# Two weighted-latent products of a latent-attention kernel formed together in every second step, both halves of the second feed-forward layer in one step

## The reference

```python
xn = layernorm(x)
# attention on xn; it normalises again, with scale and bias, to h
c_q, c_kv = h @ w_down_q.T, h @ w_down_kv.T              # 64 latents each
q, k, v = c_q @ w_up_q.T, c_kv @ w_up_k.T, c_kv @ w_up_v.T   # 16 heads of 64
q, k = rope(q), rope(k)
attn = softmax(q @ k.T / 8)                              # 256 x 256 per head
a = (attn @ v) @ w_out.T + xn
# feed-forward with a spiking neuron
y = square(relu(xn @ W_fc.T)) @ W_proj.T
spikes = number of spikes in 5 steps of mem = 0.9*mem + y - reset
out = x + a + spikes / 5
```

## Time and profile before

| | |
|---|---|
| median of 3 executions | 1122.33 us (1120.78 to 1128.31) |
| profiled execution | 1125.72 us, its span 1123.8 us |
| TensorE clock granted, mean of the span | 0.987 of full speed |
| steps | 256, and 12 before the first; 8 a batch |

### The profile page before, as it was taken

How to read it: one execution, slowest core, us unless ns; L and a number is a source line. 1 busy time by engine, 2 the same in 40 slices (tenths; PEclk the granted TensorE clock), 3 DMA queues, 4 the chain that set the end, 5 groups by cost and what they waited for, 6 DMA issues and landing times.

```text
span 1123.8 us, 26195 instructions
## 1 busy us (share of the span) xinstructions
PE 1058.6 (94%) x6880; PEld 715.4 (64%) x6880; DVE 908.0 (81%) x1222; ACT 930.4 (83%) x3137; POOL 903.2 (80%) x901
## 2 busy tenths in 40 slices
PE   3789999999999999999999999999999999999977
PEld 2555666666666666666666666666666666666644
DVE  3888788888888888888888888888888888888840
ACT  3779788888888888888888888988888888888851
POOL 3767788888888888888888888888888888977841
PEclk9989999999999999999999999999999999999997
DMA  5378678777777877777787777778777778877770
GB/s 160 114 195 213 174 198 227 198 204 198 199 203 195 230 194 201 207 194 201 198 225 197 196 210 195 201 205 215 201 196 207 199 195 216 210 199 194 197 181 19
DMA packets 93281, 217.96 MB, mean 194 GB/s; under 512 B 22464, under 2 KB 43200, under 8 KB 93120
## 3 DMA queue, kind: packets, MB, share of 16 engines
q1 hardware_dynamic: 93248, 217.57, 73.1%
HBM read 7.77 MB, written 4.19 MB: 11 GB/s over the span
## 4 chain that ended last, share of the span: by engine, by line
PE 46%; DVE 16%; ACT 15%; issue 14%; SPq 5%; DMA 2%; DVEq 1%; POOL 1%; ACTq 0%; POOLq 0%
PE ps_s L315 12%; PE ps_u L329 12%; PE ps_b L407 10%; ACT prob L483 8%; DVE neg_max L606 7%; PE ps_a L368 5%; SPq L247 4%; PE ps_qk L305 4%; ACT spread L507 2%; DVE latent L643 2%; DVE turned L615 2%; PE ps_qk L306 2%; DVE qk L601 2%; ACT raw L495 2%; ACT latent L538 1%
## 5 line engine op out<-in xcount | busy, mean ns | idle before, releaser
L483 ACT ACTIVATE prob<-ps_s,neg_max 128x256 f32<-128x256 f32 x1024 | 473.8, 484 | 95.8 <-DVE neg_max L606 94.7
L733 POOL TENSOR_TENSOR partner<-partner,rope_sb 128x512 f32<-128x512 f32 x256 | 326.8, 1276 | 140.8 <-DMA partner<-raw 136.8
L606 DVE TENSOR_REDUCE neg_max<-ps_s 128x4 f32<-128x1024 f32 x256 | 310.0, 1211 | 102.1 <-PE ps_s L315 101.1
L736 POOL TENSOR_TENSOR qk<-qk,partner 128x512 f32<-128x512 f32 x256 | 326.3, 1275 | 20.1
L615 DVE STREAM_TRANSPOSE turned<-prob 128x1024 f32<-128x1024 f32 x256 | 315.3, 1232 | 1.2 <-ACT prob L483 0.2
L315 PE MATMUL ps_s<-qk 64*128 64x256 f32 x2048 | 293.5, 406 | 1.6 <-ACT prob L483 1.1
L329 PE MATMUL ps_u<-gathered,ckv 128*64 128x256 f32 x2048 | 281.7, 396 | 11.2 <-DMA gathered<-turned 9.8
L315 PEld LDWEIGHTS ps_s<-qk 64*128 64x128 f32 x2048 | 178.3, 188 | 111.5 <-issue 90.9
L483 ACT ACTIVATION_READ_ACCUMULATOR prob<-ps_s,neg_max 128x1 f32 x1024 | 220.2, 215 | 0.0
L601 DVE TENSOR_TENSOR qk<-ps_qk,rope_sb 128x512 f32<-128x512 f32 x256 | 175.1, 684 | 41.9 <-ACT raw L495 38.9
L495 ACT COPY raw<-ps_qk 128x512 f32<-128x512 f32 x256 | 155.3, 607 | 48.8 <-PE ps_qk L306 48.5
(11 more groups left out here) (58 smaller groups left out, 900.6 us busy)
## 6 DMA issues: line engine op xcount, KB each, us to landing
gathered<-turned SPq DMA_DIRECT2D x1024, 128.0 KB, 2.4
partner<-raw SPq DMA_DIRECT2D x256, 256.0 KB, 2.3
x_sb<-in_x SPq DMA_DIRECT2D x32, 128.0 KB, 2.3
resid<-early SPq DMA_DIRECT2D x32, 128.0 KB, 2.0
out<-out_sb SPq DMA_DIRECT2D x32, 128.0 KB, 2.1
turned<-in_wup SPq DMA_DIRECT2D x2, 512.0 KB, 5.7
rope_sb<-in_rope SPq DMA_DIRECT2D x1, 512.0 KB, 6.7
turned<-in_wo_t SPq DMA_DIRECT2D x1, 512.0 KB, 8.0
```

Of the source, the lines that this page charges most:

```text
L483: last = nc.scalar.activation(prob[:, s % 2, :, h, :, t, :].rearrange("p j k c -> p k j c"), ps_s[:, s % 2, h, t, :].rearrange("p (k j c) ...
L606: nc.vector.tensor_reduce(neg_max[:, s % 2, :, :], ps_s[:, s % 2, :, :, :], AXIS_X, ALU.max, negate=True).then_inc(max_ready, 1)
L733: nc.gpsimd.tensor_tensor(other, other, sin_sb, ALU.mult).then_inc(sin_ready, 1)
L736: nc.gpsimd.tensor_tensor(qk[:, s % 4, :, :], qk[:, s % 4, :, :], other, ALU.add).then_inc(rope_done, 1)
```

## The change

`weigh_latents` and `copy_u` run in the odd steps alone, each for two pairs: 16 instructions on TensorE write both halves of ps_u, and one copy of 512 columns takes them to u_sb. The semaphores u_ready and u_evac count twos of pairs instead of pairs. `ffn_out` half 1 moves from p = 3 to p = 2, behind half 0. The waits of `move` and `normalise_u` name the same pairs in the new count. Cut to its core:

```diff
-        ps_u = pb("ps_u", [P, 512])
+        ps_u = pb("ps_u", [P, 2, S])
...
-                sp.wait_ge(u_ready, done(g - 2 * GROUP))
+                sp.wait_ge(u_ready, done(i * (BODY // 2) + s // 2 - GROUP))
...
-            def weigh_latents(g, s, i):
+            def weigh_latents(duo, s, i):
...
-                pe.wait_ge(u_evac, done(g - 1))
+                pe.wait_ge(u_evac, done(duo - 1))
...
-                for kt in range(TT):
-                    for h in range(2):
-                        last = nc.tensor.matmul(
-                            ps_u[h * L:(h + 1) * L, 0:S], ckv[:, (s // PAIRS) % 2, kt, :],
-                            gathered[:, (s // GROUP) % 2, :, s % GROUP, h, kt, :, :].rearrange("p i t r -> p t i r"),
-                            start=(kt == 0), stop=(kt == TT - 1))
+                for pair in range(s, s + 2):
+                    for kt in range(TT):
+                        for h in range(2):
+                            last = nc.tensor.matmul(
+                                ps_u[h * L:(h + 1) * L, pair % 2, :], ckv[:, (s // PAIRS) % 2, kt, :],
+                                gathered[:, (s // GROUP) % 2, :, pair % GROUP, h, kt, :, :].rearrange("p i t r -> p t i r"),
+                                start=(kt == 0), stop=(kt == TT - 1))
...
-                if not outside(b, B) and p in (2, 3):
-                    ffn_out(b, p - 2)
+                if not outside(b, B) and p == 2:
+                    ffn_out(b, 0)
+                    ffn_out(b, 1)
...
-                if not outside(g, STEPS):
-                    weigh_latents(g, s, i)
+                if s % 2 == 1 and not outside(g, STEPS):
+                    weigh_latents(i * (BODY // 2) + s // 2, s - 1, i)
...
-                nc.scalar.copy(u_sb[:, (s // PAIRS) % 2, pair, :], ps_u[:, 0:S]).then_inc(u_evac, 1)
+                nc.scalar.copy(u_sb[:, (s // PAIRS) % 2, pair:pair + 2, :], ps_u[:, :, :]).then_inc(u_evac, 1)
...
-                if not outside(g, STEPS):
-                    copy_u(g, s, i)
+                if s % 2 == 1 and not outside(g, STEPS):
+                    copy_u(i * (BODY // 2) + s // 2, s - 1, i)
...
-                pool.wait_ge(u_evac, done(PAIRS * b + 2 * c + 1))
+                pool.wait_ge(u_evac, done(CHUNKS * b + c))
```

More of the change, by code:

```diff
@@ L238, in store, with move @@
                 sp.dma_start(out_v[b], out_sb[:, par, :, :]).then_inc(stored[par], 16)
-            def move(g, s, rows_of):
+            def move(g, s, i, rows_of):
                 par = (s // GROUP) % 2
@@ L277, in step @@
                 if (s + turn) % GROUP == GROUP - 1 and not outside(g + turn, STEPS):
-                    move(g + turn, s + turn, (0,))
+                    move(g + turn, s + turn, i, (0,))
                 if (s + LEAD["project"]) % 2 == 1 and not outside(g + LEAD["project"], STEPS):
@@ L281, in step @@
                 if (s + turn) % GROUP == 0 and not outside(g + turn - 1, STEPS):
-                    move(g + turn - 1, s + turn - 1, (1, 2, 3))
+                    move(g + turn - 1, s + turn - 1, i, (1, 2, 3))
                 if p == 3:
@@ L317, in scores @@
                 last.then_inc(s_ready, 1)
-            def weigh_latents(g, s, i):
-                if isinstance(g, int) and g == 0:
+            def weigh_latents(duo, s, i):
+                if isinstance(duo, int) and duo == 0:
                     pe.wait_ge(setup_dve, 4)
@@ L423, in value_by_output @@
                             rows = slice(h * DH, (h + 1) * DH)
-                            last = nc.tensor.matmul((ps_u, ps_b)[half][h * L:(h + 1) * L, j * D:(j + 1) * D],
+                            last = nc.tensor.matmul((ps_u[:, :, :].rearrange("p j s -> p (j s)"), ps_b)[half][h * L:(h + 1) * L, j * D:(j + 1) * D],
                                                     wv_sb[rows, pair, :], wo_sb[rows, pair, :],
@@ L495, in copy_projected, with copy_u @@
                 nc.scalar.copy(raw[:, duo % 2, s % 2, :, :], ps_qk[:, :, :]).then_inc(raw_ready, 1)
-            def copy_u(g, s, i):
-                act.wait_ge(u_ready, done(g))
+            def copy_u(duo, s, i):
+                act.wait_ge(u_ready, done(duo))
                 b, pair = i * UNROLL + s // PAIRS, s % PAIRS
-                if pair % 2 == 0 and not outside(b - 2, B):
+                if not outside(b - 2, B):
                     act.wait_ge(out_part, done(CHUNKS * (b - 2) + pair // 2))
-                nc.scalar.copy(u_sb[:, (s // PAIRS) % 2, pair, :], ps_u[:, 0:S]).then_inc(u_evac, 1)
+                nc.scalar.copy(u_sb[:, (s // PAIRS) % 2, pair:pair + 2, :], ps_u[:, :, :]).then_inc(u_evac, 1)
             def copy_spread(b, c):
@@ L691, in copy_value_by_output @@
                 nc.vector.tensor_copy(sel_sb[:, :, :], sel_raw).then_inc(setup_dve, 1)
-                nc.vector.tensor_copy(wvo_sb[:, 0:PAIRS // 2, :], ps_u[:, :].rearrange("p (j d) -> p j d", d=D))
+                nc.vector.tensor_copy(wvo_sb[:, 0:PAIRS // 2, :], ps_u[:, :, :].rearrange("p j s -> p (j s)").rearrange("p (j d) -> p j d", d=D))
                 nc.vector.tensor_copy(wvo_sb[:, PAIRS // 2:PAIRS, :],
```

## The result

| | before | after |
|---|---|---|
| median | 1124.23 us (1120.78 to 1128.31, 4 runs) | 1139.65 us (1138.05 to 1140.51, 4 runs) |
| profiled span | 1123.8 us | 1138.7 us |
| a batch in the middle of the run | 32.9 us | 33.7 us |

The ratio is 1.0134, with a 95% interval of 1.0094 to 1.0174: the change makes the kernel 15 us slower. The forecast was 1140, in a range of 1126 to 1158. It had laid 18 us on a median of 1122.33; the median of the four runs compared here is 1124.23, and the measured difference is 15.4 us.

The account below looks back on a forecast made before the run. TensorE's own order of work sets the end in nearly every step. Terms 0.87 - 0.16 + 0.05 - 0.16 = +0.60 a batch, in 30 batches +18 us on 1122.33: 1140 us, range 1126 to 1158.

Parts of the forecast that it names:

- The main step, p = 0 and 1: TensorE in p = 0 and 1: L398 still starts at +5.82, waiting 1.33; pair 8.14 against 7.27 us, +0.87 a batch.
- The cost of a switch: TensorE's changes of tile form: 0.16 from weighing to scores, 0.09 into weighing; joint weighing saves 0.16 a pair of steps.
- steps 2 and 3: p = 2 and 3, with ffn_out half 1 moved into step 2: no wait, -0.16 us a batch.
- Steps 6 and 7: p = 6 and 7: L414 hangs on the last output product through L662, as before; -0.16 us a batch.
- Steps 4 and 5: p = 4 and 5: L407's wait goes, L368 waits 0.3 to 0.5 for the last L654; +0.05 us a batch.
- The joint copy: ScalarE's one copy of 512 columns for two of 256: 25 us less on ScalarE, worth nothing on TensorE's path.
- This sign of being right: On ScalarE, listed among what would show the prediction right: 25 us less busy time.
- Moved half, DMAs, and what waits for them: ffn_out half 1 in step 2 waits for nothing; DMAs keep their queue places; up to 12 waits of 0.3 go.
- Start and drain: The two ends of the run: counted at nothing, within 2 us.
- The faster one: Rival, chance 0.11: p = 0's spread copy comes at +4.4 or earlier through ScalarE's relief; -24 us, 1098 us.
- No change: Rival, chance 0.14: the switch saves 0.25 a pair and L368 does not wait; 1117 to 1131 us.
- Slower by more: Rival, chance 0.15: the run of 16 streams no better than two of 8; 1.24 a batch, 1160 us.

Follow-up runs that it names:

- the experiment on the spike counts: VectorE's three spike counts of p = 4 put ahead of that step's transposition: in the changed kernel 1118.74 us (0.9976), in the kernel before 1123.95 us (1.0005).
- the joint copy alone: Kernel before with only the copy to u_sb made joint, in the odd step; weighing stays in every step: 1123.44 us, ratio 1.0012.
- two orders mended: Changed kernel with broadcasts and spread copies earlier in p = 0 to 3 and p = 4's three spike counts ahead of the transposition: 1099.59 us, 0.9794.
- one copy earlier in either kernel: In p = 0 ScalarE makes spread copy 0 ahead of the latents' work: changed kernel 1125.95 us (1.0031), kernel before 1123.10 us (0.9996).
- all four earlier: Changed kernel with broadcasts right behind the projection and spread copies ahead of the exponentials in p = 0 to 3: 1122.55 us, ratio 0.9997.
- both orders in the kernel before: Kernel before with earlier broadcasts and spread copies in p = 0 to 3 and p = 4's spike counts ahead of the transposition: 1123.11 us, 1.0003.

## Why the prediction held

**The main step, p = 0 and 1.** +0.87 forecast, +0.86 measured. L399 starts at +5.82 after the scores as said, waits 1.18 to 1.40 for 1.33, and the pair takes 8.13 for 8.14. The argument was that L398 was already waiting in the kernel before, so TensorE had no slack to give there.

**The cost of a switch.** The run of 16 takes 1.88, as worked out, and steps 2 and 3 together fell by 0.16. Steps 6 and 7 gave 0.14. Step 4 is 2.60: its extras start at +1.64 and are four instructions of 0.86, so the entry from full-array products to the scores is 0.10, for the 0.09 taken. So the switches cost as read, 0.16 and 0.09. In the batch cut out TensorE's busy time fell by 0.62 us (32.34 to 31.72), 19 us in 30 batches. The 23 us on the pages agree less than they seem to: the six traces of kernels with weighing in every step, the same work for TensorE, show 1041.7 to 1058.6 us. The Trainium skill's gap of the streaming time and 2.5 ns (TensorE: Matmul & The Clock Gate, Back-to-back issue gap) is for a single product by itself, and has no term for a change of tile form, where the rows here say 0.16.

**Steps 4 and 5.** +0.05 forecast, +0.18 measured. The wait of L369 came where it was put, at 0.40 to 0.48 in a range of 0.3 to 0.5. The term was mis-sized by 0.13: from the row maximum to the last count VectorE took 4.42 instead of 4.19, where the rotation starts 0.12 after the row maximum has ended (648.91 after 648.79); before, the records followed each other without a gap. The prediction had taken 4.19 as the earliest, and put the whole of the wait and its restart at 0.5; by the starts it was 0.67 (the experiment on the spike counts).

**The joint copy.** Worth nothing, as said; two runs show it. But ScalarE's busy time fell by 3.8 us, not by the 25 forecast. The group itself fell from 102.4 to 78.1 us, but the records overlap, and the engine's busy time counts an overlap once (the last section). This sign of being right was wrong.

**Moved half, DMAs, and what waits for them.** Nothing, as said for both. A wait for the blocks was not seen in the changed kernel at all, the 4.3 us at the end of the run included, so the drain didn't stay as it was.

**Sum and ends.** A batch grew by 0.74 in the two cut out, and by 0.78 as a mean of 22 to 23, against 0.60. That alone would be 22 to 24 us. Laid out by the scores of p = 0, the 26 batches in the middle took 855.6 us before and 875.8 after, 20.1 more, or 0.77 each. Start and drain, counted at nothing within 2 us, gave 5.3 of that back: what lies ahead of these batches is 3.4 us shorter, what lies behind them 1.9. The start is the second batch, which took 36.86 us before and 33.94 after. The same stretch in both, the kernel before first:

```profile
102.00:120.00 18.00, 15.98 (x96) 10.30 (x96) 14.33 (x22) 12.67 (x45) 15.36 (x18) 0.91 0.71 186
```

```profile
102.00:120.00 18.00, 17.17 (x114) 11.83 (x114) 16.41 (x24) 15.64 (x54) 14.76 (x18) 1.00 0.82 213
```

Before, the weighing of p = 4 there waited 2.02 us for its blocks and the granted clock of the stretch was 0.91; behind the wait the eight weighing instructions took 1.97 us for 1.08 and the next scores 1.88 for 1.13, which is the lower of TensorE's two clock levels. After, the clock is 1.00 without that wait. By the starts of the scores of p = 0 this batch is 37.2 us before and 33.9 after. Of the five other traces with weighing in every step four show it at 35.1 to 36.7 us, and one, the joint copy alone in its fastest execution, at 33.5; the seven other traces with joint weighing show 33.4 to 34.0. So the late second batch is no accident of one execution, though each kernel has only one trace.

So the mechanism and its place are right, and the closeness of 1140 to 1139.65 is luck. The middle grew by 4.5 us more than 26 times 0.60, the four batches at the ends gave 5.3 where 2.4 had been added, which leaves 14.9 us between the spans for 18; and the median that the 18 were added to was 1.9 us lower than that of the comparison.

**The rivals.** None came true. The faster one asked for the spread copy to come earlier through ScalarE's relief; it came at the same +5.18. No change needed switches of 0.25 and no wait of L369; they cost 0.16, and L369 waits. Slower by more needed a run of 16 of 2.0 or more; it takes 1.88.

## What to carry over

Work on an engine that sets the end is not only a cost: where its next instruction already waits for another engine, it is the cover of that wait, and moving it elsewhere turns it into idle time. So look, for each place work is taken from, at the distance to the next wait, and reorder the waited-for work first; here the same change is 1.3% slower by itself and, with two orders mended, 2.1% faster than the kernel before, while those orders alone bring nothing. And a wait taken away shows the next one: four of the experiments gave half or nothing for that reason (one copy earlier in either kernel, all four earlier, and both orders in the kernel before).

## What the runs showed of the hardware that was not expected

The records of neighbours on ScalarE overlap, so the length of a record is not what the engine's busy time loses with it. The copy of 256 columns is 0.400 us on the page; counted in the traces, 58 of the 102.4 us of these copies lie under the record ahead or behind, and 20 of the 78.1 of the joint ones. With one copy in place of two in 128 places the engine was busy only 3.8 us less, not 25, and with two again in the changed kernel 6.2 us more (932.8 for 926.6). Neither figure is the price of a copy: among the kernels with the same 3009 instructions on ScalarE the busy time goes from 909.9 to 930.5 us, as the records lie closer or further apart.

Going over from one form of tile to another costs TensorE 0.09 to 0.16 us at full clock, read from the distances of starts: 0.16 from weighing to scores, 0.09 from full-array products to weighing, 0.10 from these to scores. What the engine does in that time no row shows.
